# Routed expert tiles of a fused token/attention/MoE kernel: the gathered rows are transposed by DMA instead of by TensorE

## The chip, the cores and the metric

The kernel runs on one core of a Trainium2 chip. The metric is the device time of one execution in microseconds (us), the median of three runs. A TensorE clock of 1.00 in a profile row is the full 2.4 GHz, 0.50 is 1.2 GHz.

## The reference

What is computed, cut to what matters here (3,072 rows of 512 numbers; 8 experts, two for each row):

```
h = concat(ssm_kernel(x), txt)                 # 8 x 384 rows of 512
h = h + attention(layernorm(h))                # causal, latent of 64
n = layernorm(h)
w = group_limited_top2(softmax(n @ gate.T))    # weights of 2 of 8 experts per row
routed = sum over e: w[:, e] * (silu(n @ gate_w[e].T) * (n @ up_w[e].T)) @ down_w[e].T
shared = silu(n @ sh_gate.T) * (n @ sh_up.T) @ sh_down.T
return h + routed + shared
```

## The kernel before

The program has three long stretches: the first part of the tokens (to about 125 us of the span), attention overlapped with the shared expert (to 593 us), and the routed experts (from 594 us to the end). The change is in the last.

**Number format.** Every product of large operands is made with numbers split into a high and a low float16 part, in three passes (high by high, high by low, low by high). Normalised rows were stored to DRAM earlier as `x2_dram`, 1,024 float16 a row: 512 high, 512 low.

**Routed tiles.** Rows are sorted by expert into 55 tiles (`SLOT_TILES`) of 128 rows; `SLOTS` holds for each tile its 128 row numbers and their weights. One tile goes through these steps, in order:

1. GpSimd (POOL) copies the tile's row numbers to a small buffer `G_NUM` (L2258) and issues an indirect DMA that gathers 128 rows of `x2_dram` into `X16` (L2261). There are two buffers `X16`, and the gather runs three tiles ahead (`ahead = 3`).
2. `turn_x` on TensorE: eight 128x128 transposes of the tile into a PSUM bank (L2097). `copy_x` on ScalarE copies the bank to `XT16` (L2165, two buffers). The tile after next's gather waits for `turn_x`.
3. TensorE makes the gate product (12 matmuls of 352 columns, L2087 to L2089), then the up product (12 more). Between them stands `turn_a` of the tile before (6 transposes, L2119), and behind the up product `turn_x` of the next tile, and then `down` of the tile before (9 matmuls of 512 columns).
4. ScalarE takes the SiLU (L2178); VectorE multiplies, finds each row's largest number and splits the result (L2206 to L2220); ScalarE writes the high part (L2186) and copies the transposed activations (L2171).
5. VectorE scales the down product to `YO` (L2244, two buffers). It may do so for tile t when the scatter of tile t-2 has landed (`s_added`).
6. POOL scatters `YO` with addition into the output in DRAM (L2274, an indirect DMA). Scatters of different tiles can hit the same output row, so each waits until the one before has landed (`s_add`). Behind that wait stand the copy of the row numbers to `S_NUM` (L2270), the wait for that copy, the wait for `YO`, and the issue.

POOL's order in the loop is gather(t+3), scatter(t). SyncE (SP) has nothing in this stretch after its first 2 us: it issues the load of the ninth block of weights (`s_nine`, 2.2 MB, L1821) and the last three stores of the shared part, `store(7)` (L1786). The ninth block is split into high and low parts by ScalarE and VectorE between the tiles 3 and 10. SP has issued 30 DMA transposes earlier, for the shared expert (L1776, DRAM to SBUF, 128 rows of 1,024 float16 each, the same size as a routed tile).

The first tile waits for the last low part of the weight split (`lows_done`). Its `XT16` buffers lie where staging buffers of that split were.

Of the kernel before, what the change touches and what calls it, by code (L numbers as in the profile page):

```python
# [14 lines left out]
P = 128  # L15
# [35 lines left out]
MCH = 11  # L51
# [101 lines left out]
def build(nc, a):  # L153

    with ExitStack() as ctx:
# [496 lines left out]
        ident16 = small(P // 2).bitcast(F16)  # L652
        EXPT, EOFF = small(SLOT_TILES), small(SLOT_TILES).bitcast(I32)
        SLOTS = small(SLOT_TILES, 2)
        G_NUM = [small(2).bitcast(U32) for _ in range(2)]
        S_NUM = [small(2).bitcast(U32) for _ in range(2)]
        GATE16 = small(KC * E).bitcast(F16)
        AMX, ARC = small(2), small(2)
# [9 lines left out]
        YO = [small(D) for _ in range(2)]  # L668
        assert st_at[0] <= WORK
        EXPC = cut(work, sc_at, SLOT_TILES, E)  # L670
        X = [htile(0, 2), htile(0, 5)]
        X16, XT16 = [x.bitcast(F16) for x in X], [x.bitcast(F16) for x in XT]
        def x_turned(tile, at):
            return tile[:, at:at + 3 * D].bitcast(F16).rearrange("p (t k x) -> p t k x", t=3, k=2 * KC)
# [1095 lines left out]
        def attn_sync(sp):  # L1770

            def load(b, x, s):
                for t in range(3):
                    r = 3 * b + t
                    sp.wait_ge(s_x2[r % 3], 16 * (r // 3 + 1))
                    sp.dma_start_transpose(x[:, t], x2_d[r * P:(r + 1) * P, :]).then_inc(s, 16)  # L1776

            def store_rows(b):
                for t in range(3 * b, 3 * b + 3):
                    sp.wait_ge(lg_low, t + 1)  # L1780
                    sp.dma_start(x2_d[t * P:(t + 1) * P, :], XS[t % 3]).then_inc(s_x2[t % 3], 16)
# [24 lines left out]
            store_rows(5)  # L1806
            store(2)
            store_rows(6)
            sp.wait_ge(at_p.sem, at_p.at(f"out5_{PAIRS - 1}"))
            load(6, XT_LOOK[0], s_xt_look[0])  # L1810
            store_rows(7)
            load(7, XT_LOOK[1], s_xt_look[1])
            load_turned(5)
            store(3)
            load_turned(6)
            store(4)
            load_turned(7)
            store(5)
            store(6)
            sp.wait_ge(ff_p, B * SH_UNITS)  # L1820
            sp.dma_start(big[:, SHARED0:SHARED0 + BLK], a["weights"][E - 1]).then_inc(s_nine, 16)  # L1821
            store(7)


        ro_v = steps("ro_v", [
            "lmax", "lsub", "sum", "rsum", "score", "gs"]
# [205 lines left out]
        class Moe:  # L2032
# [4 lines left out]
            def __init__(self, name, tiles, nb, per, head):  # L2037
                self.tiles, self.nb, self.units = tiles, nb, tiles * nb
                self.per, self.head = per, head
                self.tt = per // nb  # L2040
                self.turns = (self.units - head) // per
                assert head + self.turns * per + 1 == self.units and self.tt % 2 == 0
                (self.gate, self.up, self.xturn, self.down, self.aturn, self.silu, self.xcopy, self.acopy, self.mul,
                 self.top, self.top2, self.inv, self.high, self.low, self.y) = (sem(f"{name}_{k}") for k in (
                     "gate", "up", "xturn", "down", "aturn", "silu", "xcopy", "acopy", "mul",
                     "top", "top2", "inv", "high", "low", "y"))

            def run(self, eng, slot, between=None):
# [17 lines left out]

                return not isinstance(i, int) or c >= n

            def ends(self, i, c):

                return c % self.nb == self.nb - 1 and not (isinstance(i, int) and self.unit(i, c) == self.units - 1)

        routed = Moe("ro", SLOT_TILES, 1, 4, 11 + (SLOT_TILES - 4) % 4)
        s_x = [sem(f"s_x{u}") for u in range(2)]
        s_nine, nine_high, nine_low = sem("s_nine"), sem("nine_high"), sem("nine_low")

        s_gi, s_si, s_add, s_added, s_go = (sem(n) for n in ("s_gi", "s_si", "s_add", "s_added", "s_go"))

        XB, GB, UB, TBK, OB = 0, (1, 2), (3, 4), 5, (6, 7)
        big16 = big[:].bitcast(F16)  # L2080

        def moe_tensor(pe, m, offset, x_sem, between=None):
# [5 lines left out]
                pe.matmul(out, x_high, w_low, start=False, stop=False)  # L2088
                return pe.matmul(out, x_low, w_high, start=False, stop=stop)  # L2089

            def turn_x(i, t):

                pe.wait_ge(x_sem[t % 2], (i * (m.tt // 2) + (t // 2 + 1)) * 16)
                if m.from_(i, t, 1):
                    pe.wait_ge(m.xcopy, m.tile(i, t))
                for c in range(2 * KC):
                    mm = pe.transpose(PS[:, XB, :].bitcast(F16)[:, c * P:(c + 1) * P], X16[t % 2][:, c * P:(c + 1) * P], ident16)  # L2097
                mm.then_inc(m.xturn, 1)

            def product(i, c, k, wo):  # L2100

                bank, done = ((GB[c % 2], m.gate), (UB[c % 2], m.up))[k]
                x = XT16[(c // nb) % 2]
                for ch in range(KC):
                    at = (k * KC + ch) * F
                    mm = passes(PS[:, bank, 0:F], x[:, ch * P:(ch + 1) * P], x[:, (KC + ch) * P:(KC + ch + 1) * P],
                                wo(at, F, P), wo(BLK + at, F, P), ch == 0, ch == KC - 1)
                mm.then_inc(done, 1)
# [26 lines left out]

            def slot(i, c):
                wo = offset(pe, i, c)
                if c % nb == 0:
                    pe.wait_ge(m.xcopy, m.tile(i, c // nb + 1))
                if m.from_(i, c, 2):  # L2140
                    pe.wait_ge(m.silu, m.unit(i, c - 1))
                    pe.wait_ge(m.mul, m.unit(i, c - 1))
# [1 line left out]
                if m.from_(i, c, 1):  # L2144
                    turn_a(i, c - 1)
                product(i, c, 1, wo)
                if m.ends(i, c):
                    turn_x(i, c // nb + 1)
                if m.from_(i, c, 1):
                    down(i, c - 1)  # L2150

            turn_x(0, 0)
            m.run(pe, slot, between)
            turn_a(m.turns, m.head)
            down(m.turns, m.head)

        def moe_scalar(act, m, split=None):
            nb = m.nb

            def copy_x(i, t):  # L2160
                act.wait_ge(m.xturn, m.tile(i, t + 1))

                if m.from_(i, t, 2):
                    act.wait_ge(m.up, m.unit(i, (t - 1) * nb))
                act.activation(XT16[t % 2], PS[:, XB, :].bitcast(F16), ACT.Copy).then_inc(m.xcopy, 1)  # L2165

            def copy_a(i, c):
                act.wait_ge(m.aturn, m.unit(i, c + 1))
# [4 lines left out]
            def slot(i, c):  # L2173
# [4 lines left out]
                act.activation(SG[u], PS[:, GB[u], 0:F], ACT.Silu, scale=1 / (X_SCALE * W_SCALE)).then_inc(m.silu, 1)  # L2178
                if m.from_(i, c, 1):
                    copy_a(i, c - 1)  # L2180
                if m.ends(i, c):
                    copy_x(i, c // nb + 1)
                act.wait_ge(m.inv, m.unit(i, c + 1))
                if m.from_(i, c, 2):
                    act.wait_ge(m.aturn, m.unit(i, c - 1))
# [1 line left out]
                if split is not None and isinstance(i, int):  # L2187
                    split(act, i, c)

            copy_x(0, 0)  # L2190
            m.run(act, slot)
            copy_a(m.turns, m.head)

# [53 lines left out]
        def routed_gpsimd(pool):  # L2247

            def numbers(i, t):
                x = SLOTS.rearrange("p t c -> p (t c)").bitcast(U32)  # L2250
                return x[:, 2 * t:2 * t + 2] if isinstance(i, int) else x[:, bass.ds(i * 4 + t * 2, 2)]

            def gather(i, t):
                u = t % 2
                if t >= 2:

                    pool.wait_ge(routed.xturn, i * 2 + (t - 1))
                pool.tensor_copy(G_NUM[u], numbers(i, t)).then_inc(s_gi, 1)  # L2258
                pool.wait_ge(s_gi, i * 2 + (t + 1))
                pool.sem_inc(s_go, 1)  # L2260
                pool.indirect_dma_start(X16[u], None, x2_d, bass.IndirectOffsetOnAxis(ap=G_NUM[u][:, 0:1], axis=0)).then_inc(  # L2261
                    s_x[u], 16)

            def scatter(i, t):
                u = t % 2

                if t >= 1:
                    pool.wait_ge(s_add, (i * 2 + t) * 16)
                pool.sem_inc(s_added, 1)
                pool.tensor_copy(S_NUM[u], numbers(i, t)).then_inc(s_si, 1)  # L2270
                pool.wait_ge(s_si, i * 2 + (t + 1))
                pool.wait_ge(routed.y, i * 2 + (t + 1))
                pool.sem_inc(s_go, 1)
                pool.indirect_dma_start(out_d, bass.IndirectOffsetOnAxis(ap=S_NUM[u][:, 0:1], axis=0), YO[u], None,  # L2274
                                        compute_op=ALU.add).then_inc(s_add, 16)

            ahead = 3
            late = iter(ON_POOL[-6:])
            for q in late:
                if q == ON_POOL[-4]:  # L2280
# [4 lines left out]
                    gather(0, 0)  # L2285
                    gather(0, 1)
                split_low_g(pool, q)
            gather(0, 2)
            for b in range(B):
                pool.wait_ge(s_out[b], 3 * 16)  # L2290
            for t in range(2):
                gather(0, t + ahead)
                scatter(0, t)
            turns = (SLOT_TILES - ahead - 2) // 2
            with pool.Fori(0, turns) as i:
                for t in range(2, 4):
                    gather(i, t + ahead)
                    scatter(i, t)
            for t in range(2 * turns + 2, SLOT_TILES):
                if t + ahead < SLOT_TILES:  # L2300
                    gather(0, t + ahead)
                scatter(0, t)
# [28 lines left out]
        def _(act):  # L2331
            tok_scalar(act)
            attn_scalar(act)
            moe_scalar(act, routed, nine_scalar)

        @block.gpsimd
# [12 lines left out]
        def _(pe):  # L2349
# [8 lines left out]
                elif c == routed.head - 1:  # L2358
                    pe.wait_ge(nine_low, PIECES)

            moe_tensor(pe, routed, routed_offset, s_x, between)


def declare(nc, a):
# [81 lines left out]
```

## Time and profile before

| | us |
|---|---|
| median of 3 runs | 969.4 (968.99 to 970.17) |
| the profiled execution's own time | 966.46 |
| its span | 964.6 |
| mean granted TensorE clock | 0.967 |
| TensorE busy | 829.0 (86% of the span) |
| VectorE busy | 513.3 |
| ScalarE busy | 395.0 |
| GpSimd busy | 349.4 |

The span runs from the first to the last instruction. An engine's busy time counts its data instructions; waits, register work and the issue of a DMA by SP or ACT are not in it. Times on POOL are rough.

### The profile page before, as it was taken

Reading aid. Unit: us, or ns where it says so; the run is one execution under the profiler, and the core shown is the slowest. Engines: PE = TensorE matmul, PEld = TensorE weight load, DVE = VectorE, ACT = ScalarE, POOL = GpSimd, SP = SyncE. Lnnn points to the kernel's source line nnn. Section 1 sums busy time; section 2 is a strip of 40 time slices with the busy share of each in tenths; the row PEclk is TensorE's granted clock in tenths of the full one; section 3 lists DMA queues with packets and bytes.
Section 4 is the critical chain, followed back from the end, with each engine's and each line's share of the span. In section 5 each row is a group of like instructions: output and inputs, shape, how many; then the busy total and the mean of one; then the engine's idle time right before and its main releaser. Section 6 shows DMA issues by size and latency. Waiting matters only on the chain.

```text
span 964.6 us, 20136 instructions
## 1 busy us (share of the span) xinstructions
PE 829.0 (86%) x7301; PEld 522.5 (54%) x7302; DVE 513.3 (53%) x919; ACT 395.0 (41%) x683; POOL 349.4 (36%) x352
## 2 busy tenths in 40 slices
PE   0009999989799999699859997999999999999993
PEld 0009997655355545355436553666666666666661
DVE  7997746656652544736776442455434444444441
ACT  5863324334223232537442153454444444444441
POOL 0056744413810011524331032344444444444442
PEclk9999999989989999999979998999999999999996
DMA  5021234044412003597342054354444544444542
GB/s 191 0 66 47 59 111 143 24 88 121 111 45 66 1 24 108 135 225 160 92 90 80 23 153 155 79 89 83 83 79 85 87 87 76 79 85 86 87 76 33
DMA packets 66046, 84.68 MB, mean 88 GB/s; under 512 B 36096, under 2 KB 36224, under 8 KB 65344
## 3 DMA queue, kind: packets, MB, share of 16 engines
q0 software_dynamic: 12480, 29.37, 17.4%
q1 hardware_dynamic: 41408, 31.48, 11.8%
q10 hardware_dynamic: 12096, 22.94, 8.7%
q8 instruction: 46, 0.75, 0.3%
q14 instruction: 16, 0.13, 0.0%
HBM read 48.38 MB, written 27.53 MB: 79 GB/s over the span
## 4 chain that ended last, share of the span: by engine, by line
PE 72%; DVE 12%; ACT 6%; POOL 3%; issue 3%; DMA 2%; ACTq 0%; DVEq 0%; POOLq 0%
PE PS L2087 10%; PE PS L2089 10%; PE PS L2088 10%; PE PS L1075 7%; PE PS L590 6%; PE PS L1076 6%; PE PS L1077 6%; PE PS L2097 3%; PE PS L746 2%; PE PS L2119 2%; PE PS L1276 2%; PE PS L1233 1%; PE PS L2028 1%; DVE work L1422 1%; PE PS L1234 1%
## 5 line engine op out<-in xcount | busy, mean ns | idle before, releaser
L2087 PE MATMUL PS<-big,work 128*128 x605 | 200.9, 332 | 4.1 <-ACT work L2165 2.4
L2089 PE MATMUL PS<-big,work 128*128 x605 | 201.2, 333 | 0.0
L2088 PE MATMUL PS<-big,work 128*128 x605 | 201.2, 332 | 0.0
L2274 POOL DMA_INDIRECT out_dram<-work x55 | 88.0, 1600 | 62.5 <-DVE work L2244 46.0
L2206 DVE SCALAR_TENSOR_TENSOR work<-work,PS 128x352 f32<-128x352 f32 x55 | 28.7, 522 | 154.0 <-PE PS L2089 154.0
L2165 ACT ACTIVATE work<-PS 128x1024 f16<-128x1024 f16 x55 | 56.3, 1024 | 85.2 <-PE PS L2097 85.2
L2087 PEld LDWEIGHTS PS<-big,work 128*128 128x128 f16 x605 | 59.3, 98 | 42.6 <-issue 6.7
L2089 PEld LDWEIGHTS PS<-big,work 128*128 128x128 f16 x605 | 59.4, 98 | 42.2 <-issue 0.3
L2088 PEld LDWEIGHTS PS<-big,work 128*128 128x128 f16 x605 | 59.2, 98 | 36.5 <-issue 0.3
L994 POOL TENSOR_TENSOR big<-work,big 128x544 f16<-128x544 f32 (+1 forms) x30 | 38.0, 1267 | 108.8 <-ACT work L980 108.8
L2261 POOL DMA_INDIRECT big<-x_dram,work x55 | 55.8, 1015 | 46.7 <-POOL work L2258 45.0
L2178 ACT ACTIVATE work<-PS 128x352 f32<-128x352 f32 x55 | 25.5, 464 | 110.0 <-PE PS L2089 110.0
L1075 PE MATMUL PS<-big 128*128 128x384 f16 x176 | 59.6, 339 | 7.2 <-DVE big L1178 7.2
L1075 PE MATMUL PS<-big,work 128*128 128x512 f16 x144 | 56.5, 392 | 10.3 <-DVE work L1173 9.4
L1169 DVE SCALAR_TENSOR_TENSOR work<-work,PS 128x384 f32<-128x384 f32 (+1 forms) x48 | 29.5, 614 | 67.1 <-PE PS L1077 51.0
L1076 PE MATMUL PS<-work,big 128*128 128x384 f16 (+1 forms) x236 | 63.8, 291 | 0.0
L1075 PE MATMUL PS<-work,big 128*128 128x384 f16 (+1 forms) x236 | 63.6, 292 | 0.0
L1077 PE MATMUL PS<-work,big 128*128 128x384 f16 (+1 forms) x236 | 63.4, 291 | 0.0
L1154 ACT ACTIVATE work<-work 128x384 f16<-128x384 f32 (+1 forms) x48 | 24.9, 519 | 93.1 <-DVE work L1169 92.0
L590 PE MATMUL PS<-big,work 128*64 128x64 f32 x1024 | 54.8, 226 | 6.5 <-DVE big L565 6.2
L1076 PE MATMUL PS<-big 128*128 128x384 f16 x176 | 59.4, 338 | 0.0
L1077 PE MATMUL PS<-big 128*128 128x384 f16 x176 | 59.2, 337 | 0.0
(284 smaller groups left out, 1754.2 us busy)
## 6 DMA issues: line engine op xcount, KB each, us to landing
work<-in_weights ACTq DMA_DIRECT2D x36, 272.0 KB, 2.8
work<-in_shared ACTq DMA_DIRECT2D x28, 256.0 KB, 3.3
x_dram<-big SPq DMA_DIRECT2D x24, 256.0 KB, 2.3
out_dram<-big SPq DMA_DIRECT2D x24, 256.0 KB, 3.5
big<-in_weights ACTq DMA_DIRECT2D x20, 272.0 KB, 2.9
big<-in_weights SPq DMA_DIRECT2D x1, 2176.0 KB, 9.8
big<-in_par SPq DMA_DIRECT2D x1, 1185.0 KB, 10.7
big<-in_c_real SPq DMA_DIRECT2D x1, 1024.0 KB, 5.8
```

The lines of the kernel that those rows point to most:

```text
L590: mm = pe.matmul(out, power[:, h * PW:(h + 1) * PW], coeff[:, h * 64:(h + 1) * 64], start=(k == 0), stop=(k == 3))
L994: pool.tensor_tensor(piece_out(q, 1), stage(q), piece_out(q, 0), ALU.subtract).then_inc(sp_low_g, 1)
L1075: pe.matmul(out, a_high, b_high, start=start, stop=False)
L1076: pe.matmul(out, a_high, b_low, start=False, stop=False)
L1077: return pe.matmul(out, a_low, b_high, start=False, stop=stop)
L1169: v.scalar_tensor_tensor(x, x, KSC[r, :], PS[r, bank_of(n), 0:S], ALU.mult, ALU.mult).then_inc(ff_mul, 1)
L2087: pe.matmul(out, x_high, w_high, start=start, stop=False)
L2088: pe.matmul(out, x_high, w_low, start=False, stop=False)
L2089: return pe.matmul(out, x_low, w_high, start=False, stop=stop)
L2165: act.activation(XT16[t % 2], PS[:, XB, :].bitcast(F16), ACT.Copy).then_inc(m.xcopy, 1)
L2261: pool.indirect_dma_start(X16[u], None, x2_d, bass.IndirectOffsetOnAxis(ap=G_NUM[u][:, 0:1], axis=0)).then_inc(s_x[u], 16)
L2274: pool.indirect_dma_start(out_d, bass.IndirectOffsetOnAxis(ap=S_NUM[u][:, 0:1], axis=0), YO[u], None, compute_op=ALU.add).then_inc(s_add, 16)
```

## The change

- `turn_x` and `copy_x` go. SP transposes each gathered tile by a DMA from SBUF to SBUF (`turn_rows`), and TensorE waits for that DMA's semaphore `s_xr`.
- There are four `X16` and four `XT16` buffers. `turn_rows` of tile t waits for the gather of t and for the up product of tile t-4. The gather of t waits for the transpose of t-4, and gathers run five tiles ahead.
- The first transposes carry waits of their own: tile 0 for the end of the weight split, tile 2 and 3 for the shared expert's last units. `store(7)` stands between the transposes of tiles 1 and 2 on SP's queue. The load of the ninth block moves from SP's queue to ACT's.
- The copy of the row numbers to `S_NUM` moves ahead of the wait for the scatter before.
- Gathers 2 to 4 wait for the last gate and up units of the shared expert, since their buffers lie on its input. The loop of POOL is unrolled to four tiles.

```diff
-        X = [htile(0, 2), htile(0, 5)]
+        X = [cut(big, HT0 + slot_of(0, 2) * D + u * D, D) for u in range(4)]
+        XT = [XT[0], cut(work, x_at, D), cut(big, XT1_AT + 2 * D, D), XT[1]]
...
-            sp.wait_ge(ff_p, B * SH_UNITS)
-            sp.dma_start(big[:, SHARED0:SHARED0 + BLK], a["weights"][E - 1]).then_inc(s_nine, 16)
+            for t in range(2):
+                turn_rows(sp, t)
             store(7)
+            for t in range(2, 4):
+                turn_rows(sp, t)
+            for t in range(4, SLOT_TILES):
+                turn_rows(sp, t)
+
+        def turn_rows(sp, t):
+            u = t % 4
+            sp.wait_ge(s_x[u], (t // 4 + 1) * 16)
+            if t == 0:
+                lows_done(sp)
+            if t == 2:
+                sp.wait_ge(ff_p, (B - 1) * SH_UNITS + MCH)
+            if t == 3:
+                sp.wait_ge(ff_p, B * SH_UNITS)
+            if t >= 4:
+                sp.wait_ge(routed.up, t - 3)
+            sp.dma_start_transpose(XT16[u].rearrange("p (k x) -> p k x", k=2 * KC), X16[u]).then_inc(s_xr[u], 16)
...
-                if c % nb == 0:
-                    pe.wait_ge(m.xcopy, m.tile(i, c // nb + 1))
+                pe.wait_ge(x_sem[c % 4], (i + c // 4 + 1) * 16)
...
                 product(i, c, 1, wo)
-                if m.ends(i, c):
-                    turn_x(i, c // nb + 1)
                 if m.from_(i, c, 1):
                     down(i, c - 1)
...
                     copy_a(i, c - 1)
-                if m.ends(i, c):
-                    copy_x(i, c // nb + 1)
...
             def gather(i, t):
-                u = t % 2
-                if t >= 2:
-
-                    pool.wait_ge(routed.xturn, i * 2 + (t - 1))
+                u = t % 4
+                if t >= 4:
+                    pool.wait_ge(s_xr[u], (i + t // 4) * 16)
...
             def scatter(i, t):
                 u = t % 2
-
+                pool.tensor_copy(S_NUM[u], numbers(i, t)).then_inc(s_si, 1)
                 if t >= 1:
-                    pool.wait_ge(s_add, (i * 2 + t) * 16)
+                    pool.wait_ge(s_add, (i * 4 + t) * 16)
                 pool.sem_inc(s_added, 1)
-                pool.tensor_copy(S_NUM[u], numbers(i, t)).then_inc(s_si, 1)
-                pool.wait_ge(s_si, i * 2 + (t + 1))
-                pool.wait_ge(routed.y, i * 2 + (t + 1))
+                pool.wait_ge(s_si, i * 4 + (t + 1))
+                pool.wait_ge(routed.y, i * 4 + (t + 1))
                 pool.sem_inc(s_go, 1)
...
-            ahead = 3
+            ahead = 5
...
             attn_scalar(act)
+            act.wait_ge(ff_p, B * SH_UNITS)
+            act.dma_start(big[:, SHARED0:SHARED0 + BLK], a["weights"][E - 1]).then_inc(s_nine, 16)
             moe_scalar(act, routed, nine_scalar)
```

## Rows read from the trace of the kernel before

**Rows 1.** The page, part 4: the chain that ended last, shares by engine

```profile
PE 72%; DVE 12%; ACT 6%; POOL 3%; issue 3%; DMA 2%; ACTq 0%; DVEq 0%; POOLq 0%
```

**Rows 2.** Windows: stretch, its us, busy us of PE, PEld, DVE, ACT, POOL, clock, DMA share, GB/s

```profile
594.00:604.00 10.00, 6.69 (x42) 4.07 (x43) 2.18 (x6) 2.75 (x4) 1.18 (x2) 0.83 0.94 314
640.00:928.00 288.00, 287.29 (x2135) 182.09 (x2133) 126.32 (x281) 129.30 (x187) 136.45 (x184) 1.00 0.49 84
```

**Rows 3.** Timeline (start us, us, instruction, idle before): TensorE around one tile's transposes, and one idle spot

```profile
702.43 0.31 PE L2089 MATMUL PS<-big,work 128*128 x1
702.58 0.61 PE L2097 MATMUL PS<-work,big 128*128 128x128 f16 x8
703.03 0.38 PE L2087 MATMUL PS<-big,work 128*128 x1
...
712.15 0.32 PE L2087 MATMUL PS<-big,work 128*128 x1 [0.71 <-issue]
```

**Rows 4.** Timeline: GpSimd through one tile, with VectorE's write of the next YO

```profile
700.88 0.18 POOL L2270 COPY work<-work 128x2 uint32 x1 [2.17 <-DMA out_dram<-work]
...
701.94 1.60 POOL L2274 DMA_INDIRECT out_dram<-work  x1 [0.88 <-POOL work L2270]
...
704.57 1.01 POOL L2261 DMA_INDIRECT big<-x_dram,work  x1 [0.82 <-POOL work L2258]
...
705.55 0.81 DVE L2244 TENSOR_SCALAR work<-PS,work 128x512 f32<-128x512 f32 x1
...
707.04 0.18 POOL L2270 COPY work<-work 128x2 uint32 x1 [1.46 <-DMA out_dram<-work]
...
708.19 1.60 POOL L2274 DMA_INDIRECT out_dram<-work  x1 [0.97 <-POOL work L2270]
```

**Rows 5.** Timeline: a scatter that YO released

```profile
649.41 0.81 DVE L2244 TENSOR_SCALAR work<-PS,work 128x512 f32<-128x512 f32 x1
...
651.05 1.60 POOL L2274 DMA_INDIRECT out_dram<-work  x1 [0.93 <-DVE work L2244]
```

**Rows 6.** The scatter's line (ns min/median/max, first and last start)

```profile
L2274 POOL DMA_INDIRECT out_dram<-work x55: 1557/1602/1639, 612.4 to 953.5; - x55
```

**Rows 7.** The line of the copy behind the scatter's wait: what ended its idle time

```profile
  DMA out_dram<-work: 81.1, 54
```

**Rows 8.** Timeline: SP's queue, one group of three DMA transposes with nothing beside it

```profile
291.49 3.93 SPq L1776 DMA_TRANSPOSE big<-x_dram  x3
```

**Rows 9.** DMA view of 291.5:302 (packets, MB, share of 16 engines), which holds only those three

```profile
q1 hardware_dynamic: 3168, 0.79, 37.4%
```

**Rows 10.** DMA view of 291.49:297.89: busy tenths of the 16 engines, 0.16 us a digit

```profile
DMA  0000000024579999632799999531399999296000
```

**Rows 11.** The same of 701.94:708.34, from one scatter's issue on

```profile
DMA  0000000000000999393349999858637479630000
```

**Rows 12.** The line of the DMA transposes: issue to landing, all 30

```profile
DMA to landing us min/median/max: 3.2/4.2/8.7
```

**Rows 13.** The gather's line: issue to landing

```profile
DMA to landing us min/median/max: 3.3/3.6/7.4
```

**Rows 14.** The page, part 6: plain loads of 272 KB, all 20 of one kind, us to landing

```profile
big<-in_weights ACTq DMA_DIRECT2D x20, 272.0 KB, 2.9
```

**Rows 15.** DMA view of 501.3:501.5 and of 446.2:446.4: such loads while transposes ran

```profile
big<-in_weights ACTq DMA_DIRECT2D x1, 272.0 KB, 4.4
...
big<-in_weights ACTq DMA_DIRECT2D x1, 272.0 KB, 4.0
```

**Rows 16.** Timeline: the start of the routed stretch

```profile
593.43 0.34 SPq L1821 DMA_DIRECT2D big<-in_weights  x1
...
594.10 0.71 DVE L989 SCALAR_TENSOR_TENSOR big<-work,big 128x544 f16<-128x544 f32 x1
594.92 0.61 PE L2097 MATMUL PS<-work,big 128*128 128x128 f16 x8 [1.52 <-issue]
...
603.80 0.32 PE L2087 MATMUL PS<-big,work 128*128 x1 [1.20 <-ACT work L2165]
```

More of the change, by code:

```diff
@@ L654, in build @@
         SLOTS = small(SLOT_TILES, 2)
-        G_NUM = [small(2).bitcast(U32) for _ in range(2)]
+        G_NUM = [small(2).bitcast(U32) for _ in range(4)]
         S_NUM = [small(2).bitcast(U32) for _ in range(2)]
@@ L670, in build @@
         EXPC = cut(work, sc_at, SLOT_TILES, E)
-        X = [htile(0, 2), htile(0, 5)]
+        X = [cut(big, HT0 + slot_of(0, 2) * D + u * D, D) for u in range(4)]
+        XT = [XT[0], cut(work, x_at, D), cut(big, XT1_AT + 2 * D, D), XT[1]]
+        assert HT0 + slot_of(0, 2) * D + 2 * D == XT1_AT
         X16, XT16 = [x.bitcast(F16) for x in X], [x.bitcast(F16) for x in XT]
@@ L2042, in __init__ @@
                 assert head + self.turns * per + 1 == self.units and self.tt % 2 == 0
-                (self.gate, self.up, self.xturn, self.down, self.aturn, self.silu, self.xcopy, self.acopy, self.mul,
+                (self.gate, self.up, self.down, self.aturn, self.silu, self.acopy, self.mul,
                  self.top, self.top2, self.inv, self.high, self.low, self.y) = (sem(f"{name}_{k}") for k in (
-                     "gate", "up", "xturn", "down", "aturn", "silu", "xcopy", "acopy", "mul",
+                     "gate", "up", "down", "aturn", "silu", "acopy", "mul",
                      "top", "top2", "inv", "high", "low", "y"))
@@ L2067, in from_ @@
                 return not isinstance(i, int) or c >= n
-            def ends(self, i, c):
-                return c % self.nb == self.nb - 1 and not (isinstance(i, int) and self.unit(i, c) == self.units - 1)
         routed = Moe("ro", SLOT_TILES, 1, 4, 11 + (SLOT_TILES - 4) % 4)
-        s_x = [sem(f"s_x{u}") for u in range(2)]
+        s_x, s_xr = [sem(f"s_x{u}") for u in range(4)], [sem(f"s_xr{u}") for u in range(4)]
         s_nine, nine_high, nine_low = sem("s_nine"), sem("nine_high"), sem("nine_low")
         s_gi, s_si, s_add, s_added, s_go = (sem(n) for n in ("s_gi", "s_si", "s_add", "s_added", "s_go"))
-        XB, GB, UB, TBK, OB = 0, (1, 2), (3, 4), 5, (6, 7)
+        GB, UB, TBK, OB = (1, 2), (3, 4), 5, (6, 7)
         big16 = big[:].bitcast(F16)
@@ L2089, in passes @@
                 return pe.matmul(out, x_low, w_high, start=False, stop=stop)
[L2091 to L2098, printed above, removed]
             def product(i, c, k, wo):
                 bank, done = ((GB[c % 2], m.gate), (UB[c % 2], m.up))[k]
-                x = XT16[(c // nb) % 2]
+                x = XT16[c % 4]
                 for ch in range(KC):
@@ L2146, in slot @@
                 product(i, c, 1, wo)
-                if m.ends(i, c):
-                    turn_x(i, c // nb + 1)
                 if m.from_(i, c, 1):
                     down(i, c - 1)
-            turn_x(0, 0)
             m.run(pe, slot, between)
@@ L2158, in moe_scalar @@
             nb = m.nb
[L2160 to L2165, printed above, removed]
             def copy_a(i, c):
@@ L2188, in slot @@
                     split(act, i, c)
-            copy_x(0, 0)
             m.run(act, slot)
@@ L2250, in numbers @@
                 x = SLOTS.rearrange("p t c -> p (t c)").bitcast(U32)
-                return x[:, 2 * t:2 * t + 2] if isinstance(i, int) else x[:, bass.ds(i * 4 + t * 2, 2)]
+                return x[:, 2 * t:2 * t + 2] if isinstance(i, int) else x[:, bass.ds(i * 8 + t * 2, 2)]
             def gather(i, t):
-                u = t % 2
-                if t >= 2:
-                    pool.wait_ge(routed.xturn, i * 2 + (t - 1))
+                u = t % 4
+                if t >= 4:
+                    pool.wait_ge(s_xr[u], (i + t // 4) * 16)
                 pool.tensor_copy(G_NUM[u], numbers(i, t)).then_inc(s_gi, 1)
-                pool.wait_ge(s_gi, i * 2 + (t + 1))
+                pool.wait_ge(s_gi, i * 4 + (t + 1))
                 pool.sem_inc(s_go, 1)
@@ L2287, in routed_gpsimd @@
                 split_low_g(pool, q)
-            gather(0, 2)
+            pool.wait_ge(ff_p, (B - 1) * SH_UNITS + MCH)
+            for t in range(2, ahead):
+                gather(0, t)
             for b in range(B):
                 pool.wait_ge(s_out[b], 3 * 16)
-            for t in range(2):
+            for t in range(4):
                 gather(0, t + ahead)
                 scatter(0, t)
-            turns = (SLOT_TILES - ahead - 2) // 2
+            turns = (SLOT_TILES - ahead - 4) // 4
             with pool.Fori(0, turns) as i:
-                for t in range(2, 4):
+                for t in range(4, 8):
                     gather(i, t + ahead)
                     scatter(i, t)
-            for t in range(2 * turns + 2, SLOT_TILES):
+            for t in range(4 * turns + 4, SLOT_TILES):
                 if t + ahead < SLOT_TILES:
@@ L2359, in between @@
                     pe.wait_ge(nine_low, PIECES)
-            moe_tensor(pe, routed, routed_offset, s_x, between)
+            moe_tensor(pe, routed, routed_offset, s_xr, between)
 def declare(nc, a):
```

## The prediction

> **What bounds the kernel now.** I read the chain that ended last first: TensorE holds 72% of it [rows 1]. Then the windows of the routed stretch, where the whole change lies: in 288 us TensorE is busy 287.29 us at full clock, while GpSimd is busy 136 us, ScalarE 129 us, VectorE 126 us and the 16 DMA engines 0.49 of the time [rows 2]. So TensorE sets the pace. The 54 steps from the first scatter at 612.4 to the last at 953.5 [rows 6] make 341.1 / 54 = 6.317 us a tile.
>
> Busy shares hide a second loop that is almost as long. The reader should follow GpSimd through one tile [rows 4]: the scatter starts at 701.94, its landing releases the copy at 707.04 (5.10 us later), the copy takes 0.18 us, and 0.97 us more pass before the next scatter starts at 708.19: 6.25 us for the round. Over all tiles, the idle time that a landing ended is 81.1 us in 54 waits [rows 7], 1.50 us each; GpSimd had finished its gather at 2.63 + 1.01 = 3.64 us after the scatter's start [rows 4], so landing takes 5.14 us on average. The second tick to note is that YO was ready at 705.55 + 0.81 = 706.36, before the landing. TensorE's loop and the scatter loop differ by about 0.1 us; each scatter waits for the one before, and nothing overlaps two of them.
>
> **Transposes off TensorE.** The eight transposes start at 702.58 and the next product at 703.03 [rows 3]: 0.45 us a tile, 24.8 us over 55 tiles. TensorE's loop becomes 6.317 - 0.45 = 5.87 us. ScalarE's copy of 1.02 us goes too; it lies beside TensorE's products and is worth nothing in the steady loop.
>
> **The copy ahead of the wait.** Before, from landing to scatter: 0.18 + 0.88 to 0.97 us, 1.06 to 1.15 us [rows 4]. One could book all of it as saved. But look at a scatter that YO released [rows 5]: YO ends at 649.41 + 0.81 = 650.22 and the scatter starts at 651.05, 0.83 us later, with the copy done at 650.12. So about 0.83 us pass between the last wait and the start whatever released it, and only the copy's 0.2 us goes. I take 0.89 us from landing to start (0.83 and the semaphore step behind the landing); the ends are 0.1 (all of it saved) and 1.0 us. The scatter loop becomes 5.14 + 0.89 = 6.03 us. That is more than TensorE's 5.87: **the scatter loop becomes the bound**, and without anything else it gives 54 x (6.03 - 6.317) = -15.5 us.
>
> **The DMA transposes.** The trace has 30 of the same size, from DRAM, none from SBUF. Three alone issue in 3.93 us, 1.31 us each [rows 8], take 37.4% of 10.5 us = 3.93 us of all 16 engines, again 1.31 us each [rows 9], and land in 3.2 to 8.7 us, median 4.2 [rows 12]. Four buffers give each about three tiles of time, 17 us, so their own time is covered, and TensorE does not wait for them. What they do to the scatters is the open price.
>
> Where do they fall? A gather starts 2.63 us after a scatter [rows 4] and lands 3.6 us later [rows 13], at 6.23; the up product that the transpose also waits for (of tile t+1 when the gather of t+5 lands) is older, because it precedes the YO that released the scatter. So the transpose is issued at 6.3. Its traffic begins 8 digits of 0.16 us, 1.3 us, after the issue and lasts 1.4 us [rows 10]: 7.6 to 9.0. Counted from the next scatter, which starts at 6.03, that is 1.5 to 3.0 us. The scatter's traffic runs from 2.1 to about 4.9 us after its start, at less than half load in the first microsecond [rows 11]. They overlap for 0.8 to 0.9 us, every tile, and in a fixed phase: gather data follow the scatter's, so a later landing also makes the transpose later.
>
> How much is the scatter delayed? Below: nothing, if its thin first part fits in the gaps. Above: the whole 1.31 us. Nearest rows: a 272 KB load lands in 2.9 us [rows 14], and in 4.0 and 4.4 us among transposes [rows 15]; its own data need about 0.8 us of all engines (at the 314 / 0.94 = 334 GB/s of the first window of [rows 2]; an estimate). So a load that lay wholly under transposes was stretched by 1.1 to 1.5 us, to 0.35 to 0.4 of its rate. The scatter needs about half of the engines in the overlap and gets perhaps a third to a half: it falls behind by 0.1 to 0.5 us. I take 0.3. The loop is 6.03 + 0.3 = 6.33 us: 54 x (6.33 - 6.317) = +0.7 us.
>
> The Trainium skill (Advanced Engine Details and Errata, X-Bar Transpose) says that transposing DMAs on trn2 are as fast as regular ones. Here the trace differs: 256 KB at the load's rate above need 0.8 us of the engines, a transpose took 1.31 us. By that rule the burst would be all but over as the scatter's data begin, and the sum would be the -15.5 us without collision.
>
> **The start.** Now TensorE's first transposes start at 594.92, just after the last weight split (594.10 + 0.71), and TensorE is ready for the second tile's gate at 603.80, after a wait of 1.20 us for ScalarE's copy [rows 16]; the clock was 0.83 there [rows 2]. After: the transpose of tile 0 waits for the same split, so it is issued at about 594.9 and lands 3.2 us later at best. But it shares the engines with the 2.2 MB load, now on ACT's queue, in a window of DMA share 0.94 [rows 2]; the gather issued there landed in 7.4 us, not 3.6 [rows 13], so +3.8 us is the other end: 598.1 to 602.5. Then 24 matmuls (24 x 0.15 = 3.6 us by the starts in [rows 3]) and 1.7 us lost to the clock, as before (0.17 of 10 us): second gate at 603.5 to 607.9, against 603.80. Less the 0.45 of tile 2's transposes, the first scatter moves by -0.7 to +3.7 us; I take +1.5. The load's move to ACT costs 0.34 us of its queue under the wait; `store(7)` behind two transposes (2.6 us) has until the first scatter at 612.4. Nothing for either. Gathers five ahead cost the same instructions as three ahead, and the tail after the last scatter (11 us) stays.
>
> **Sum.** +0.7 + 1.5 = +2.2 us on the profiled execution's own 966.46: 968.7. The median of the runs is 2.9 us above that execution, so 971.6; I say 972.
>
> **Rivals.** All are 966.46 + 1.5 + 54 x (loop - 6.317) + 2.9.
> - *Scatter-bound, hardly any collision* (delay under 0.1): loop 6.03, 955. For it: DMA share rises only to (0.49 x 6.317 + 1.31) / 6.03 = 0.73. Against: loads among transposes were late every time [rows 15].
> - *Scatter-bound, heavy collision* (delay 0.5 to 1.31 us): loop 6.83 at a delay of 0.8 gives 998, at 1.31 1026. For it: the transposes hold the engines like nothing else in the trace. It decides from a delay of 0.25 us on: beyond that the kernel is slower than before.
> - *TensorE stays the bound*: landing to start is short (0.1 us), and the collision under 0.6: loop 5.87, 946. Against: [rows 5].
> - *Transposes themselves become the bound*: from SBUF, or one at a time, they could be slower than any row; each serial at the slowest landing of 8.7 us gives a loop of 8.7 and 1100. Against: 1.31 us of issue pace. The Trainium skill (VectorE: DVE Perf Modes, The three transpose paths) gives the DMA crossbar 1,309 ns for one 128x128 block against TensorE's 390 ns, and advises TensorE; eight blocks in a row by that figure would be 10.5 us a tile. Rows here show 1.31 us for all eight, so the trace does not agree in a stream.
> - *TensorE's clock falls*, as it would wait 0.46 us a tile. A pause of 0.71 us was followed by a matmul at full speed (0.32 us) [rows 3], so I leave it at nothing.
>
> **Chances.** Partial collision (delay 0.1 to 0.5, 961 to 983) 0.50; hardly any 0.20; heavy 0.20; TensorE-bound 0.07; transposes too slow 0.03. A change under 0.2% (1.9 us) can't be told from none. Faster by more needs a delay under 0.22: 0.20 + 0.07 + 0.15 of the partial case = 0.42. Within it: 0.22 to 0.29, 0.10. Slower: 0.25 + 0.20 + 0.03 = 0.48. The range 952 to 998 leaves out the TensorE-bound case, the upper half of heavy, and the slow transposes, 0.07 + 0.10 + 0.03 = 0.20.
>
> **What would show it.** Right: scatters 6.2 to 6.5 us apart, nearly all released by POOL's wait on the landing and not by VectorE; landing about 0.3 us later than 5.14; landing to start 0.8 to 0.9 us; TensorE with idle time of some 0.4 us a tile that ends with VectorE or ScalarE. Wrong: TensorE idle before L2087 ended by the transpose's semaphore; scatters 5.9 us apart; a first product after 603; a clock below 1.00 in the loop.

## The result and the profile after

The changed kernel takes 989.96 us (median of 4 runs, 983.04 to 997.18) against 969.78 us: ratio 1.0201, 95% interval 1.016 to 1.0242. It is slower by about 2%, and its four runs spread over 14 us. They spread with the mean granted TensorE clock: 0.962 at 983.04 us, 0.957 at 989.13, 0.955 at 990.80 and 0.951 at 997.18. The profiled execution is the fastest of the four, 983.04 us, 16.6 us above the one profiled before. The numbers of the traces explain those 16.6 us.

The page of the changed kernel, part 4 (shares of the span in the chain that ended last), which answers to [rows 1]:

```profile
PE 38%; DMA 32%; DVE 13%; ACT 6%; issue 6%; POOL 3%; POOLq 1%; ACTq 0%; DVEq 0%; SPq 0%
DMA out_dram<-work 29%; PE PS L1077 7%; PE PS L590 6%; PE PS L1078 6%; PE PS L1079 6%; PE PS L748 2%; PE PS L1278 2%; PE PS L1235 1%; PE PS L2046 1%; DVE work L2235 1%; DVE work L1424 1%; PE PS L1236 1%; DVE work L1175 1%; ACT work L1156 1%; DMA work<-big 1%
```

Before, TensorE held 72% of it and DMA 2%. Now one kind of transfer, the scatters into the output, holds 29%, about 285 of 981 us; no line of the routed products is left among those that the page names. The windows of the routed loop (same columns as [rows 2], whose row is 640 to 928):

```profile
650.00:960.00 310.00, 286.56 (x1851) 165.19 (x1849) 129.35 (x290) 90.02 (x147) 138.81 (x184) 1.00 0.67 115
```

TensorE is idle for 23.4 of 310 us, the DMA share rose from 0.49 to 0.67, and the clock stayed at 1.00. The scatter's own line (answers to [rows 6]; the last row is issue to landing):

```profile
L2263 POOL DMA_INDIRECT out_dram<-work x55: 1557/1600/1658, 618.0 to 970.0; - x55
...
DMA to landing us min/median/max: 4.6/5.5/6.1
```

(970.0 - 618.0) / 54 = 6.52 us a tile, where the kernel before took 6.317. The chain in order of time shows what one step is made of (start us, us, what):

```profile
716.25 5.51 DMA out_dram<-work
...
721.99 0.59 issue
722.58 0.05 POOLq L2248
...
722.79 5.79 DMA out_dram<-work
```

Landing at 721.76, next start at 722.79: 5.51 us of transfer and 1.03 us of GpSimd's queue. That is the whole period, 6.54 us. A reader of the waits must be careful here:

```profile
DVE work L2235 <- POOLq L2259: 134.1, 45, 4.9
POOL out_dram L2263 <- issue: 83.0, 30, 3.3
POOL out_dram L2263 <- DVE work L2235: 51.9, 17, 10.1
```

The middle row says "issue" although the landing was waited for: other queue instructions lie between that wait and the DMA, so the landing is no longer the event just before it. The first row is the real sign: L2259 is the step that tells VectorE that a `YO` buffer is free, and it comes right behind the landing. The third row names VectorE's `YO`, but it is no sign of another bound. In the step before the one above, the landing came at 715.22 in the same chain, and the scatter started at 716.25, 1.03 us later as here; VectorE's write, itself released by L2259, ended at 716.24.

Where the transposes fall (timeline, SP's and GpSimd's queues):

```profile
716.40 8.08 SPq L1841 DMA_TRANSPOSE work<-big  x2
...
718.89 1.01 POOL L2251 DMA_INDIRECT big<-x_dram,work  x1 [0.84 <-POOL work L2248]
...
722.79 1.60 POOL L2263 DMA_INDIRECT out_dram<-work  x1 [2.69 <-issue]
```

The transpose is issued 0.15 us after the scatter at 716.25. (In 40 of the 54 steps one is issued 0 to 0.6 us after the scatter, in six at 6.4 to 6.9 us, just ahead of the next.) The 16 engines' busy tenths from that scatter's start on, 0.16 us a digit (answers to [rows 11]):

```profile
DMA  0000000038999999999589557999983693697441
```

At the 9th digit (1.3 us) the transpose's burst begins; it lasts about 1.4 us, to the 17th or 18th (2.8 us). Before, the scatter's first data came at the 14th digit, 2.1 us. Now the engines are full of the transpose at that moment.

### The profile page after: what moved, and what is told of

It is laid out like the page before. It is cut to its first block, busy times and chain, and to the rows that moved or that the text cites. A ratio compares the mean times of both kernels' runs of the same rounds, so it can differ in the third digit from the quotient of the medians.

```text
span 981.2 us, 19111 instructions
## 1 busy us (share of the span) xinstructions
PE 809.9 (83%) x6861; PEld 493.0 (50%) x6862; DVE 513.3 (52%) x919; ACT 342.5 (35%) x628; POOL 351.7 (36%) x352
## 4 chain that ended last, share of the span: by engine, by line
PE 38%; DMA 32%; DVE 13%; ACT 6%; issue 6%; POOL 3%; POOLq 1%; ACTq 0%; DVEq 0%; SPq 0%
DMA out_dram<-work 29%; PE PS L1077 7%; PE PS L590 6%; PE PS L1078 6%; PE PS L1079 6%; PE PS L748 2%; PE PS L1278 2%; PE PS L1235 1%; PE PS L2046 1%; DVE work L2235 1%; DVE work L1424 1%; PE PS L1236 1%; DVE work L1175 1%; ACT work L1156 1%; DMA work<-big 1%
## 5 line engine op out<-in xcount | busy, mean ns | idle before, releaser
L2101 PE MATMUL PS<-big,work 128*128 x493 | 166.2, 337 | 11.2 <-DMA work<-big 10.2
L2103 PE MATMUL PS<-big,work 128*128 x493 | 166.3, 337 | 0.0
L2102 PE MATMUL PS<-big,work 128*128 x493 | 166.2, 337 | 0.0
L2235 DVE TENSOR_SCALAR work<-PS,work 128x512 f32<-128x512 f32 x55 | 44.5, 808 | 134.1 <-POOLq L2259 134.1
L2178 ACT ACTIVATE work<-work 128x352 f16<-128x352 f32 x55 | 32.3, 588 | 192.0 <-DVE work L2208 186.9
L2101 PEld LDWEIGHTS PS<-big,work 128*128 128x128 f16 x493 | 48.5, 98 | 45.8 <-issue 12.6
L2103 PEld LDWEIGHTS PS<-big,work 128*128 128x128 f16 x493 | 48.5, 98 | 36.7 <-issue 0.6
L2102 PEld LDWEIGHTS PS<-big,work 128*128 128x128 f16 x493 | 48.4, 98 | 33.6 <-issue 0.3
L590 PE MATMUL PS<-big 128*64 128x64 f32 x1024 | 55.9, 225 | 1.0 <-issue 1.0
```

The costliest lines, as they stand in the source:

```text
L590: mm = pe.matmul(out, power[:, h * PW:(h + 1) * PW], coeff[:, h * 64:(h + 1) * 64], start=(k == 0), stop=(k == 3))
L2101: pe.matmul(out, x_high, w_high, start=start, stop=False)
L2235: nc.vector.tensor_scalar(YO[u], PS[:, OB[u], :], AMX[:, u:u + 1], at_tile(SLOTS[:, :, 1], i, t), ALU.mult, ALU.mult).then_inc(routed.y, 1)
```

## The experiments

Loop is the distance from the first to the last scatter over 54; landing is the median from a scatter's issue to its landing, and empty where the trace gives none. The times of the kernel before that ran beside them had medians of 969 to 972 us.

| | time us | ratio to before | loop | landing |
|---|---|---|---|---|
| before | 969.78 | 1 | 6.317 | |
| changed | 989.96 | 1.0201 (1.016 to 1.0242) | 6.52 | 5.5 |
| e1 transposes behind a landing | 952.42 | 0.9797 (0.9748 to 0.9845) | 5.86 | 4.8 |
| e2 first transposes ahead of the load | 984.22 | 1.0145 (1.0093 to 1.0198) | 6.54 | 5.5 |
| e3 transposes into the scatter's body | 965.08 (one run) | | 6.18 | |
| e4 half transposes | 965.47 (one run) | | 6.09 | |
| e5 = e1 + e2 | 949.73 | 0.9759 (0.9732 to 0.9787) | 5.86 | 4.8 |
| e6 copy back behind the wait | 996.75 | 1.0274 (1.0249 to 1.0299) | 6.65 | 5.4 |
| e7 before + copy ahead | 965.94 | 0.9965 (0.9943 to 0.9987) | 6.30 | 4.8 |
| e8 scatters without addition | 952.9 (one run) | | 5.82 | 3.4 |
| e9 = e5, copy back | 962.42 | 0.9927 (0.9893 to 0.9961) | 6.12 | |
| e10 plain copies for transposes | 960.24 (one run) | | 5.99 | 5.0 |

The theory: the scatter loop bounds the changed kernel, and a transpose that is released by its gather's landing always bursts where the next scatter's data should begin. Rivals: the extra traffic as such; TensorE waiting for transposes; the queue time between landing and scatter.

**e1, move the bursts.** The same transposes, released by a scatter's landing:

```diff
             if t >= 4:
                 sp.wait_ge(routed.up, t - 3)
+            if t >= 5:
+                sp.wait_ge(s_add, (t - 4) * 16)
```

> The transpose of tile t also waits until the scatter of tile t-5 has landed, about 5.5 us after that scatter's start, so that its traffic (1.1 us after the issue, 1.4 us long in the changed kernel's trace) falls between the gather's data and the next scatter's. Same work, one more wait. Collision theory: scatters land 5.1 to 5.2 us after their start as before the change, the loop is 5.14 + 0.95 = 6.1 us and the span falls by 54 x (6.52 - 6.1) = 23 us against the changed kernel's profiled 981, to about 958; median about 963 to 967. Rival, more DMA traffic as such (wherever it falls) slows the scatters: landing stays at 5.6, loop 6.5, time about 985. Rival, the wait starves TensorE: idle time before the gate product ended by the transpose.

The time fell by 37.5 us against the changed kernel and lies 2% under the kernel before; 963 to 967 us was expected. The timeline of e1:

```profile
749.59 1.60 POOL L2265 DMA_INDIRECT out_dram<-work  x1 [1.91 <-issue]
...
754.25 1.23 SPq L1843 DMA_TRANSPOSE big<-big  x1
```

The transpose now starts 4.7 us after the scatter, so that its burst is over before the next scatter's data. The busy tenths from 749.59 on:

```profile
DMA  0399999994000997899917996307943589402999
```

The first burst (2nd to 10th digit) ends 1.6 us after the scatter's issue, the scatter's data start at the 14th as before, and the next burst begins at the right edge. The scatter's line:

```profile
L2265 POOL DMA_INDIRECT out_dram<-work x55: 1557/1600/1639, 625.1 to 941.6; - x55
...
DMA to landing us min/median/max: 4.6/4.8/5.1
```

and its window of 620:930 (columns as in [rows 2]):

```profile
620.00:930.00 310.00, 310.00 (x2065) 188.16 (x2063) 147.35 (x326) 96.91 (x167) 160.07 (x202) 1.00 0.73 128
```

The landing is 0.7 us shorter than in the changed kernel with exactly its traffic (one transpose a tile; DMA share 0.73, higher than 0.67). So it is not the amount of traffic. The loop went below the 6.1 us that I expected, to 5.86: TensorE's own, which is busy for 310.00 of 310 us. VectorE, which waited 45 times for a free `YO` in the changed kernel, does so never in e1. I had taken the undisturbed landing as 5.14, and it is 4.8.

The loops give 54 x 0.66 = 36 us; the two profiled executions differ by only 28, since the routed stretch began 7 us later in e1's. The last weight split ended at 593.87 in the changed kernel's trace and at 601.19 in e1's, in the part of the program that both share word for word. The windows of 200:250 show where most of it comes from, first the changed kernel, then e1:

```profile
200.00:250.00 50.00, 47.29 (x251) 24.94 (x252) 27.13 (x59) 21.69 (x50) 17.97 (x17) 0.90 0.31 83
200.00:250.00 50.00, 47.13 (x228) 24.87 (x227) 25.83 (x54) 21.69 (x49) 13.43 (x13) 0.76 0.31 83
```

TensorE is busy for 47 of 50 us in both, at a granted clock of 0.90 and of 0.76: an estimate of 50 x 0.14 = 7 us of work less. All the traces sort by it: with 0.90 in this window (before, changed, e2, e3, e6) the last split ends at 593.9 to 595.2, with 0.76 or 0.77 (e1, e4, e5, e8, e10) at 599.5 to 601.2; e7 and e9, with 0.86 and 0.83, lie between. Why the clock there differs from one execution to the next stays open; the loops are free of it, at a clock of 1.00.

**e2, the start.**

```diff
             act.wait_ge(ff_p, B * SH_UNITS)
+            act.wait_ge(s_xr[1], 16)
             act.dma_start(big[:, SHARED0:SHARED0 + BLK], a["weights"][E - 1]).then_inc(s_nine, 16)
```

> Only the load of the ninth block is moved behind the landing of the transposes of tiles 0 and 1. Theory: in the changed kernel the first transposes shared the engines with that 2.2 MB load and took 7.5 us to issue; alone they issue in 1.3 us each and tile 0's lands after 4, at 598, so the first product starts about 4.5 us earlier than 602.7, the first scatter at 613.5 instead of 618.0; the loop stays at 6.5 and the span falls by 4 to 5 us. Rival: the transposes from SBUF are slow on their own at the start, or the start is hidden by the scatter loop: no change.

The start of the changed kernel, timeline (answers to [rows 16]):

```profile
592.49 0.33 ACTq L2326 DMA_DIRECT2D big<-in_weights  x1
593.15 0.72 DVE L991 SCALAR_TENSOR_TENSOR big<-work,big 128x544 f16<-128x544 f32 x1
593.93 7.53 SPq L1841 DMA_TRANSPOSE work<-big  x2
...
602.70 0.47 PE L2101 MATMUL PS<-big,work 128*128 x1 [10.24 <-DMA work<-big]
```

and that of e2:

```profile
594.44 0.71 DVE L991 SCALAR_TENSOR_TENSOR big<-work,big 128x544 f16<-128x544 f32 x1
595.22 2.61 SPq L1841 DMA_TRANSPOSE work<-big  x2
...
598.53 0.47 PE L2101 MATMUL PS<-big,work 128*128 x1 [4.79 <-DMA work<-big]
```

From the end of the last split to the first product: 8.8 us in the changed kernel, 3.4 us in e2. Behind the 2.2 MB load the two transposes took 7.53 us to issue, and TensorE waited 10.24 us. The first scatter comes 24.1 us after the split (618.0 - 593.9) in the changed kernel, 19.6 in e2 (614.7 - 595.15), 17.6 in the kernel before (612.4 - 594.81). Of the 5.4 us that the first product gains the first scatter keeps 4.5: in e2 TensorE's first products run at half clock for 5.3 us, in the changed kernel for 3.5. As expected the loop did not change (6.54). The median fell by 5.7 us, where 4 to 5 were expected; the intervals of the two ratios touch (1.0093 to 1.0198 against 1.016 to 1.0242), so that it is the traces that show the gain.

**e3, bursts in the scatter's body.**

```diff
+            if t >= 6:
+                sp.wait_ge(s_go, 2 * t - 2)
```

> The transpose of tile t waits instead until the gather of tile t+1 is issued, 2.6 us after the start of scatter t-5, so that its traffic (from 3.7 to 5.1 us after the scatter's start) falls into the body of a scatter's and delays the gather's. Collision theory: the burst of 1.3 us lies wholly under the scatter's traffic: landing 5.7 to 6.4 us, loop 6.65 to 7.3, span 988 to 1024. Rival, traffic as such: as in the changed kernel, 6.5. Rival, only the scatter's first data are sensitive: landing back at 5.2, loop 6.1.

This expectation failed: a landing of 5.7 us or more and a loop of 6.65 or more were forecast. The loop is 6.18 us, (952.1 - 618.2) / 54, better than the changed kernel's. The steps fall into two kinds, as the timeline shows:

```profile
713.17 1.60 POOL L2265 DMA_INDIRECT out_dram<-work  x1 [3.20 <-DVE work L2237]
...
720.23 1.60 POOL L2265 DMA_INDIRECT out_dram<-work  x1 [3.21 <-issue]
...
726.07 1.60 POOL L2265 DMA_INDIRECT out_dram<-work  x1 [2.00 <-issue]
...
731.97 1.60 POOL L2265 DMA_INDIRECT out_dram<-work  x1 [2.06 <-issue]
```

7.06 us, then 5.84 and 5.90: of the 54 steps 12 took 6.8 us or more, and 37 took 5.5 to 6.2. Eleven of the 12 long steps had a transpose issued 1.9 to 2.3 us after the scatter, but so had 13 short ones; of the 21 steps whose transpose came later than that, one was long. So a burst under the body cost about 1 us in 11 of the 28 steps that had it issued at 1.9 to 2.3 us, and hardly ever when it came later. Why one of the 28 is long and another short is not settled. "A collision costs its overlap" is thus too simple; what the changed kernel does, a burst where the scatter's first data should go out, is dearer than one in the middle.

**e4, half the burst** (one run; from tile 4 on the low halves of the rows are left untransposed, so the pass that uses them works on stale numbers):

```diff
-            sp.dma_start_transpose(XT16[u].rearrange("p (k x) -> p k x", k=2 * KC), X16[u]).then_inc(s_xr[u], 16)
+            n = 2 * KC if t < 4 else KC
+            sp.dma_start_transpose(XT16[u].rearrange("p (k x) -> p k x", k=2 * KC)[:, 0:n], X16[u][:, 0:n * P]).then_inc(s_xr[u], 16)
```

> From tile 4 on only the high half of the columns is transposed (the low half of the turned rows is stale, so the output is not the reference's): bursts of half the work, 0.65 us, at the same place. Collision theory: the delay of 0.45 us a tile falls to 0 to 0.2: loop 6.1 to 6.3 us, span 958 to 970. Rival, a cost per DMA whatever its size: loop stays at 6.5.

Loop 6.09 us, (952.4 - 623.6) / 54. The transposes were issued 0.4 us after the scatters, as before, so they did not move; the price fell with their size, from 0.66 to 0.23 us above TensorE's 5.86. A fixed cost per DMA is out.

**e10, plain copies of the same bytes** (nothing is transposed):

```diff
-            sp.dma_start_transpose(XT16[u].rearrange("p (k x) -> p k x", k=2 * KC), X16[u]).then_inc(s_xr[u], 16)
+            sp.dma_start(XT16[u], X16[u]).then_inc(s_xr[u], 16)
```

> The changed kernel with plain DMA copies of the same 256 KB from SBUF to SBUF, with the same waits, in place of the transposes (the rows are not transposed, so the output is not the reference's). If the price is the engine time of a transpose (1.3 us of all 16 engines): a copy takes 0.8 us or less, scatters land 4.9 to 5.1 us after their start instead of 5.5, loop 5.9 to 6.1, span 957 to 966. Rival, any DMA of that size in that phase costs the same: landing 5.5, loop 6.5, span 980.

The DMA view of 650:900 of e10, and then that of the changed kernel (packets, MB, share of 16 engines in 250 us):

```profile
q1 hardware_dynamic: 6048, 11.01, 11.9%
...
work<-big SPq DMA_DIRECT2D x30, 256.0 KB
big<-big SPq DMA_DIRECT2D x11, 256.0 KB
```

```profile
q1 hardware_dynamic: 40128, 9.97, 21.3%
...
work<-big SPq DMA_TRANSPOSE x28
big<-big SPq DMA_TRANSPOSE x10
```

The 11.01 MB are 42 copies of 256 KB and the 9.97 MB 38 transposes. A copy takes 0.119 x 250 / 42 = 0.71 us of all engines, a transpose 0.213 x 250 / 38 = 1.40 us for the same 256 KB. In the same place the copies leave the landing at 5.0 and the loop at 5.99. The Trainium skill (Advanced Engine Details and Errata, X-Bar Transpose) has transposes as fast as regular DMAs; in these two runs they take twice the engine time, and the measurement decides. Half the bytes (e4) and half the time per byte (e10) buy about the same.

**e8, scatters that overwrite** (they don't add, so the output is incomplete): `compute_op=ALU.add` left out.

> The changed kernel with scatters that overwrite instead of add (the output is not the reference's): the same bytes out, no read of the destination. Theory: a landing without the read is 1 us or more shorter, the scatter loop falls under TensorE's 5.87 us, and the loop is 5.87, span about 946, with TensorE busy for all of it: the gain of the transposes' removal is there and the scatter loop hides it. Rival, TensorE itself is slowed by waiting for transposes: loop stays above 6.2.

The scatter's line and the window of e8:

```profile
L2263 POOL DMA_INDIRECT out_dram<-work x55: 969/982/994, 624.5 to 938.7; - x55
...
DMA to landing us min/median/max: 2.7/3.4/5.6
```

```profile
620.00:930.00 310.00, 310.00 (x2065) 188.55 (x2064) 147.13 (x326) 97.28 (x167) 121.18 (x203) 1.00 0.50 128
```

TensorE is busy for 310.00 of 310 us. Most of the steps between scatters are 5.86 us; the last one, 3.8 us, brings the loop's mean to 5.82. TensorE's gain of 0.45 us was there all the time, behind the scatters, and it never waits for a transpose in the loop. The run says nothing of the collision: with the loop shorter, most of its transposes are issued 5.2 to 5.5 us after a scatter and no longer beside it.

**e6, e7 and e9, the copy of the row numbers**, behind or ahead of the wait in three kernels. e6 and e9 move it back behind `s_added` in the changed kernel and in e5; e7 is the kernel before with only this part of the change:

```diff
             def scatter(i, t):
                 u = t % 2
+                pool.tensor_copy(S_NUM[u], numbers(i, t)).then_inc(s_si, 1)
                 if t >= 1:
                     pool.wait_ge(s_add, (i * 2 + t) * 16)
                 pool.sem_inc(s_added, 1)
-                pool.tensor_copy(S_NUM[u], numbers(i, t)).then_inc(s_si, 1)
```

> The changed kernel with the copy of the row numbers put back behind the scatter's wait. Theory: the scatter loop is the bound there and the copy lies on it: its 0.2 us come back, loop 6.7 instead of 6.5, 54 x 0.2 = 11 us slower, median about 1000. Rival, all of the 1.06 us from landing to start comes back: 54 x 0.9, about 1035. Rival, the copy was hidden: 990.

> The kernel before with the copy of the row numbers ahead of the scatter's wait and nothing else. Theory: TensorE is the bound there (loop 6.31 us), the scatter loop just below it, so the copy's place changes nothing: ratio 0.998 to 1.000. Rival, the two loops alternate as the bound and the slack counts: 2 to 5 us faster.

> The fastest version so far (transposes behind the landing of scatter t-5, ninth block behind the first transposes) with the copy of the row numbers put back behind the scatter's wait. There the scatter loop is 4.8 + 1.0 = 5.8 us, just under TensorE's 5.86. Theory: with 0.2 us more the scatter loop is 6.0 and bounds again: 54 x 0.14 = 8 us slower, about 957. Rival, TensorE's slack covers it: 950.

e6: 6.8 us slower than the changed kernel in the median, 0.13 us a tile in the loop, somewhat under the 0.2 expected. e9: 12.7 us slower than e5 where 8 were expected, 6.12 against 5.86 a tile; the scatter loop is the bound again.

e7 is 0.35% faster than before by the medians, where I expected at most 0.2% and the rival 2 to 5 us. But most of that is the clock and not the copy. Six of e7's ten runs have a mean granted clock of 0.969, against one of the 17 of the kernel before beside it. At that clock the kernel before, in all its series, took 965.2 to 967.5 us (six runs, median 965.7) and e7 964.9 to 967.3 (median 965.2). The loops differ by 0.02 us a tile, 1 us in all. So the expectation held, and the rival's 2 to 5 us are not shown. Which loop is ahead does change with the copy's place: in the kernel before 15 scatters were released by the copy, and in e7 VectorE's YO releases 49 of 55.

**e5, what the runs point to.** e1 and e2 together:

> Both edits that helped: the transpose waits for the landing of scatter t-5, and the ninth block's load waits for the first two transposes. By the single results (952.4 and 984.2 against 990.0) the second is worth 4.5 us and lies in the start alone, so the two add: loop 5.86 us, first scatter 19.5 us after the last weight split instead of 24, median 947 to 949, 0.977 of the kernel before. Rival, the start's gain is lost again further on: 952.

949.73 us, 2.4% faster than the kernel before and 4% faster than the changed one. The window:

```profile
620.00:930.00 310.00, 308.87 (x2055) 187.32 (x2052) 147.19 (x326) 96.93 (x168) 160.37 (x204) 1.00 0.73 129
```

TensorE is the bound again, at its shorter loop. Of e2's 5.7 us 2.7 are left in the median, and the intervals of e1 and e5 overlap: the median lies between the 947 to 949 expected and the rival's 952. In the traces the gain at the start is whole: the first scatter comes 19.6 us after the last split in e5 (620.3 - 600.7) and 23.9 in e1 (625.1 - 601.2), with the same loop.

## Why the prediction was right, and where it was off

The direction came out and so did the path, the scatter loop with a transpose in its way. The size did not. +2.2 us was forecast on the profiled execution and +16.6 measured, 972 and 990 in the median. The forecast called slower by hardly more than a coin toss (0.48 against 0.42 for faster), and its range of 952 to 998 reaches to both sides of the kernel before. That the single number had the right sign is partly luck: it was +0.7 from the loop and +1.5 from the start, and two errors in it nearly cancelled.

- **The bound changes to the scatter loop.** Right for the changed kernel, and shown: the chain, e8 and e1. Wrong in its reason: the prediction had 6.03 us for the scatter loop without any collision, already above TensorE's 5.87. In e1, with the bursts moved, it is 4.8 + 1.03 = 5.83 us, and TensorE is the bound. So it is the collision that makes the scatter loop the bound, and without it the loops would have given 54 x (5.86 - 6.317) = -24.7 us and not -15.5.
- **TensorE's loop of 5.87.** Measured 5.86 in e1 and e5, and in most steps of e8.
- **Only 0.2 us of the copy's 1.06 us is saved.** Right in kind. From landing to start takes 1.03 us in the chain, where I took 0.89; e6 and e9 put the copy at 0.13 and 0.26 us.
- **The transpose falls where the next scatter's data begin, in fixed phase.** Right: forecast 0.27 us after the scatter, measured 0 to 0.6 in 40 of 54 steps. e1 and e4 show that place and size of the burst make the price.
- **The price of the collision.** I took 0.3 us on a landing of 5.14; the landing is 5.5 with the collision and 4.8 without, a price of 0.7. The two errors nearly cancel (5.44 forecast, 5.5 measured). The 5.14 was read at the copy's start behind the landing; e7, the kernel before with only the copy moved, lands in 4.8. The 0.3 rests on a misreading too: [rows 11] was read as less than half load in the scatter's first microsecond, but its six digits from the 14th on are 9, 9, 9, 3, 9, 3, a mean of 0.7. The part that was to fit into the gaps is not thin. That this alone makes the price 0.7 is not shown.
- **The loop.** It was forecast at 6.33 and is 6.52: 54 x 0.19 = 10 us, of which the queue time is 54 x 0.14 = 7.6.
- **The start.** This was the worst-sized term. I gave -0.7 to +3.7 us and took 1.5; the first scatter is 5.6 us later (618.0 against 612.4), and 6.5 if counted from the last split. I had added the delay that a gather suffered under the 2.2 MB load once; but two transposes stood in the load's way and took 7.53 us to issue, and the first landed after 8.63 us.
- **Sum.** 5.6 + 54 x (6.519 - 6.317) = 16.5 us, and the profiled executions differ by 16.6. The median of the changed kernel lies 7 us above its profiled execution; the other three runs have lower mean granted clocks (0.957 to 0.951 against 0.962), but no trace shows where in them.
- **The cases.** The likeliest case, a delay of 0.1 to 0.5 us and 961 to 983 us, is not the one that came. The delay of 0.7 us and the 990 us both belong to the heavy collision, which had a chance of 0.20. Its loop would have been 6.03 + 0.7 = 6.73 by the prediction's terms; it is 6.52, since the undisturbed loop is 5.83.
- **Nothing for the clock in the loop, for SP, for the transposes' own time**: all as forecast; clock 1.00 in the loop, and no wait for a transpose past the first.

## What to carry to other kernels

When an engine's work is moved to a DMA, compare the engine's loop with every loop of waits that is nearly as long, not with busy shares: here the second loop was 0.1 us behind the first, and with a transfer in that loop's way 0.45 us saved on TensorE became a loss. If a serial chain of DMAs then sets the pace, ask at which phase of it each other transfer bursts, and release that transfer by an event of the chain itself; here one added wait turned 2% slower into 2% faster. And at a change of stage, keep a multi-megabyte load behind the small transfers that the first product waits for.

## What the runs showed of the hardware

- A DMA transpose from SBUF to SBUF of 128 rows of 1,024 float16 issues in 1.23 us, its traffic begins about 1.1 us after the issue and lasts 1.4 us; it takes 1.40 us of all 16 engines against 0.71 us for a plain copy (e10).
- A scatter with addition of 256 KB lands in 4.8 us undisturbed (e1, e7), 3.4 us without the addition (e8; issue 1.60 against 0.98 us), and 5.5 us when a transpose's burst lies on its first data.
- A transpose issued 1.9 to 2.3 us after a scatter, so that it bursts in its middle, went with a step about 1 us longer in 11 of 28 cases; issued later than that, in 1 of 21 (e3). What decides it is open.
- The shared part of the program ended up to 7 us apart between these executions (last split at 593.9 to 601.2), and the granted clock in 200:250 goes with it: 0.90 at the early end, 0.76 at the late one. What sets it is open.
